# A decoder layer's cross-attention keys, from tokens on partitions to channels on partitions

## The reference, cut to what matters

```python
k = (encoder_hidden_states @ Wk + bk).reshape(b, se, NKV, HD).transpose(0, 2, 1, 3)   # NKV 4, HD 128
def _rmsnorm(x, w, eps=EPS):
    var = jnp.mean(xf * xf, axis=-1, keepdims=True)
    return (xf * jax.lax.rsqrt(var + eps)).astype(x.dtype) * w
k = _rmsnorm(k, kn_w)
scores = jnp.einsum('bhsd,bhed->bhse', q, k) * scale
```

## Time and profile before

| | |
|---|---|
| median of 3 runs | 1507.34 us (1504.46 to 1509.42) |
| the profiled execution, its own time | 1511.84 us |
| its span | 1510.0 us |
| PE busy | 1404.4 us, 93% of the span |
| DVE, ACT, POOL busy | 862.4 (57%), 715.8 (47%), 612.9 (41%) us |
| self-attention, about | 0 to 436 us of the span |
| cross-attention, about | 436 to 1290 us |
| one batch of the cross-attention | 51.2 us |

### The profile page before, as it was taken

The page is one execution under the profiler, slowest core; times in us unless marked ns, Lnnn a source line. Parts: engine busy times, 40 slices in busy tenths (PEclk is TensorE's granted clock), DMA queues, the critical chain, the costliest instruction groups (busy, mean ns, idle before and its releaser), DMA issues. The chain is left out here.

```text
span 1510.0 us, 24824 instructions
## 1 busy us (share of the span) xinstructions
PE 1404.4 (93%) x8553; PEld 1180.6 (78%) x8553; DVE 862.4 (57%) x3010; ACT 715.8 (47%) x1885; POOL 612.9 (41%) x936
## 2 busy tenths in 40 slices
PE   7889999999987999999999999999999997499976
PEld 7678988887866788888888888888888886377854
DVE  2644353434346676667666766676667665743357
ACT  3655555556335444445444544444444445343246
POOL 1221211212116455455545554555455436344164
PEclk9999999999999999999999999999999999599998
DMA  6211111212434221222122212212221221675363
GB/s 197 90 34 45 66 60 63 77 34 67 141 124 119 58 66 37 64 59 57 46 64 59 58 46 64 56 48 58 58 58 37 73 66 68 229 214 161 107 220 106
DMA packets 70548, 126.57 MB, mean 84 GB/s; under 512 B 11835, under 2 KB 47007, under 8 KB 69528
## 3 DMA queue, kind: packets, MB, share of 16 engines
q1 hardware_dynamic: 65848, 110.04, 23.9%
q0 software_dynamic: 4576, 14.95, 3.5%
HBM read 93.50 MB, written 31.45 MB: 83 GB/s over the span
## 5 line engine op out<-in xcount | busy, mean ns | idle before, releaser
L1341 POOL TENSOR_TENSOR b_pcarry<-b_half 128x1 f32<-128x1 f32 x173 | 49.2, 284 | 370.7 <-DVE b_rinv L1204 347.4
L75 PE MATMUL bank<-b_kTh,b_q 128*100 128x362 f32 x512 | 171.4, 336 | 8.2 <-POOL b_q L1362 6.1
L1085 ACT ACTIVATE b_probs<-b_probs,b_nmax 100x361 f32<-100x361 f32 x256 | 152.0, 594 | 18.9 <-DVE b_nmax L1198 18.6
L1198 DVE CUSTOM_DVE_ANT_0 b_probs<-bank,b_mask 100x361 f32<-100x361 f32 x256 | 135.3, 529 | 44.5 <-issue 40.0
L1373 POOL TENSOR_SCALAR b_probs<-b_probs,b_rinv 100x361 f32<-100x361 f32 x256 | 148.2, 590 | 0.0
L1080 ACT ACTIVATE b_pTh<-bank 121x400 fp32r<-121x400 f32 x192 | 96.8, 505 | 101.7 <-PE bank L917 96.9
L1191 DVE TENSOR_TENSOR b_pTl<-bank,b_pTh 121x400 fp32r<-121x400 f32 x192 | 109.6, 571 | 56.9 <-ACT b_pTh L1080 56.9
L1133 ACT ACTIVATE b_oTh<-bank,b_bv 128x400 fp32r<-128x400 f32 x64 | 38.1, 595 | 211.3 <-PE bank L75 211.3
L431 ACT ACTIVATE a_probs<-a_probs,a_nmax 100x100 f32<-100x100 f32 x256 | 93.2, 367 | 46.8 <-DVE a_nmax L551 46.7
L917 PE MATMUL bank<-ident,b_probs 100*121 100x100 f32 x768 | 110.6, 266 | 4.4 <-POOL b_probs L1373 3.5
L917 PEld LDWEIGHTS bank<-ident,b_probs 100*121 100x121 f32 x768 | 108.2, 187 | 6.6 <-POOL b_probs L1373 4.4
(11 more groups left out here) (255 smaller groups left out, 3871.0 us busy)
## 6 DMA issues: line engine op xcount, KB each, us to landing
q_d<-a_qb SPq DMA_DIRECT2D x64, 200.0 KB, 2.3
b_q_raw<-q_d SPq DMA_DIRECT2D x64, 200.0 KB, 2.4
b_q_raw<-rs_d SPq DMA_DIRECT2D x64, 200.0 KB, 3.4
b_ctxr<-in_ctxT SPq DMA_DIRECT2D x48, 242.0 KB, 4.8
y_d<-c_y SPq DMA_DIRECT2D x32, 256.0 KB
c_Eraw<-in_expert_w SPq DMA_DIRECT2D x10, 512.0 KB, 6.8
a_stage<-in_Wq SPq DMA_DIRECT2D x4, 1024.0 KB
stage<-in_Wo SPq DMA_DIRECT2D x8, 512.0 KB, 4.6
```

The costliest lines, as they stand in the source:

```text
L75: mm = eng.matmul(out, lhsT=l(c), rhs=r(c), start=first and k == 0, stop=last and k == n - 1)
L1085: act.activation(p, p, ACT.Exp, scale=-1.0, bias=nmax[:, s % 2, h:h + 1], accum_out=psums[:, s % 2, h:h + 1]).then_inc(e_rdy, 1)
L1198: dve.tensor_tensor_reduce(out=probs[:, s % 2, h, 0:SE], in0=s_bank[h % 2][0:S, 0:SE], in1=mask_s[:], scale=-1.0, scalar=BIG, op0=ALU.add, ...
L1341: pool.tensor_tensor(pcarry[:, k:k + 1], half_s[:, 0:1], half_s[:, 0:1], ALU.add)
```

## The change

It makes the keys with channels on partitions. For each of the four key heads, 128 columns of `Wk` are stationary and the context of all three chunks, 362 columns, moves: 4 heads of 12 products. The context's halves are laid out so that the three chunks adjoin. The steps are then:

- PE: head 0 at the end of slot 1, heads 1 and 2 in the quarters of slot 2, head 3 behind them; `key_sums` at the end of slot 2 sums the squares of the four heads over the partitions with a column of ones into four strips of bank 5. There are no key transposes, and the first score of each slot waits for one head of keys instead of all.
- DVE: `key_bias` moves each head from PSUM to SBUF with its bias; `key_newton` (two instructions, slot 3) makes a Newton step on the root; `key_scale` multiplies each head by the spread roots; `keys_lo`. Heads 0 and 1 of batch j+1 are scaled in slot 3, heads 2 and 3 in slots 0 and 1 of batch j+1 itself.
- ACT: `key_square` per head; `key_root` (Ln, Exp, Square; first in slot 3); `keys_hi` per head; `context_hi`, moved here from POOL, for chunks 0 to 2 behind the exponents of heads 0 to 2 in slot 1.
- POOL: no powers and no high halves; `context_lo` of all three chunks between `normalise(j, 0)` and `normalise(j, 1)`.
- SP: `spread_key_roots` behind `load_q(4j+4)`: four stores of one row each to DRAM, a wait until they have landed, and four loads that spread one row each over 128 partitions.

In the self-attention the query roots get the same Newton step (one more ACT and two DVE instructions for every four heads), the sums of squares go into bank 5 and stand behind the fourth query head, and PE's wait for the logarithm ahead of the output product is replaced by one for the Newton step ahead of every fourth query head. The queries' scale takes in the factor that the Newton steps leave. The keys of batch 0 are made at the end of the self-attention as before, in the new layout; seven dummy products ahead of a transpose in the first batch go with it. Bias, buffers and semaphores are changed to suit and are not all shown.

```diff
...
+                if m % XG == XG - 1 and XG <= m <= TAIL:
+                    pe.wait_ge(nw_set, m // XG)
...
-                if ss_bank(u) is not bank[6]:
-                    pe.wait_ge(ln_set, u - 1)
+                if ss_bank(u) is bank[5]:
+                    pe.wait_ge(sq_set, XG * u + XG + 2)
+                else:
+                    pe.wait_ge(sq_set, XG * u + XG)
+                    pe.wait_ge(nw_set, u - 1)
                 for r in range(XG):
-                    mm = pe.matmul(ss_bank(u)[r * SHD:(r + 1) * SHD, 0:GT], lhsT=ones_s[:], rhs=qsq[:, (XG * u + r) % SQ],
+                    mm = pe.matmul(ss_bank(u)[r * SHD:(r + 1) * SHD, 0:GT], lhsT=ones_s[:], rhs=square_tile(XG * u + r),
...
-                if m[0] is not None:
-                    square_sums(m[0] // XG)
                 if m[3] is not None:
                     query_head(m[3])
                 if m[0] is not None:
-                    pe.wait_ge(ln_set, m[0] // XG + 1)
+                    square_sums(m[0] // XG)
...
                     act.wait_ge(ss_done, (m - SQ) // XG + 1)
-                act.activation(qsq[:, m % SQ], q_bank(m)[:, 0:GT], ACT.Square, bias=bq_s[:, m % XH:m % XH + 1]).then_inc(sq_set, 1)
+                act.activation(square_tile(m), q_bank(m)[:, 0:GT], ACT.Square, bias=bq_s[:, m % XH:m % XH + 1]).then_inc(sq_set, 1)
             def roots(u):
...
+            def newton(u):
+                dve.wait_ge(rt_set, u + 1)
+                dve.scalar_tensor_tensor(out=qrt[:], in0=ss_bank(u)[:, 0:GT], scalar=rms_eps_s[:, 0:1], in1=qrt[:],
+                                         op0=ALU.add, op1=ALU.mult).then_inc(nw_set, 1)
+                dve.wait_ge(nw_set, u + 1)
+                dve.scalar_tensor_tensor(out=qrs[:], in0=qrt[:], scalar=-3.0, in1=qrs[:], op0=ALU.add, op1=ALU.mult).then_inc(qrs_set, 1)
...
+            def spread_key_roots(jn):
+                sp.wait_ge(k_rs, jn + 1)
+                for kv in range(XKV):
+                    sp.dma_start(kr_d[jn, kv].unsqueeze(0), krs[kv * SHD:kv * SHD + 1, :]).then_inc(krs_out, 16)
+                sp.wait_ge(krs_out, 16 * XKV * (jn + 1))
+                wait(sp, k_rdy, XKV * jn)
+                for kv in range(XKV):
+                    sp.dma_start(krb[:, kv], kr_d[jn, kv].partition_broadcast(P)).then_inc(k_in[kv], 16)
...
                     load_q(4 * j + 4, 0, 16 * j + 12)
+                    spread_key_roots(j + 1)
...
+            def keys(jn, kv, chunks=range(DC)):
                 if chunks[0] == 0:
-                    pe.wait_ge(ctx_lo, 3 * jn + c + 1)
-                    if c < 2:
-                        wait(pe, v_lo, 3 * (jn - 1) + c + 2)
-                    elif not (isinstance(jn, int) and jn == 0):
-                        pe.wait_ge(k_ev, 3 * jn + 2)
-                mm = product3(pe, key_bank(jn, c)[0:KT, :], lambda i: ctxh[:, c, i, :],
-                              lambda i: ctxl[:, c, i, :], lambda i: Wkh[:, i, :], lambda i: Wkl[:, i, :],
+                    if kv == 0:
+                        pe.wait_ge(ctx_lo, 3 * (jn + 1))
+                        pe.wait_ge(v_lo, 3 * jn)
+                    if kv >= 2:
+                        pe.wait_ge(k_sq_set, 4 * jn + kv - 1)
...
+            def key_sums(jn):
+                pe.wait_ge(k_sq_set, XKV * (jn + 1))
                 for kv in range(XKV):
-                    mm = pe.transpose(kv_bank[KEY_T_BANK[c]][:, kv * KT:(kv + 1) * KT],
-                                      kn[:, c % 2, kv * XHD:(kv + 1) * XHD], ident_s[0:KT, 0:KT])
-                mm.then_inc(kt_done, 1)
+                    mm = pe.matmul(kv_bank[0][kv * SHD:(kv + 1) * SHD, 0:SEQ], lhsT=ones_s[:], rhs=k_sq[:, jn % 2, kv, 0:SEQ],
...
                     if s >= 2 and first:
                         pe.wait_ge(w_lo, KV_PIECES + 2 * (s - 1))
                     if s == 2:
+                        if not last:
+                            keys(j + 1, 3)
                         output(j, 0, range(1))
-                        if not last:
-                            transpose_keys(j + 1, 0)
-                            if first:
-                                values_product(n - 1, s - 1, j)
-                            keys(j + 1, 2)
                     if s == 3:
                         output(j, 1, range(1, 2))
-                    if before and not (first and s == 2):
+                    if before:
                         values_product(n - 1, (s + 3) % 4, j)
+                    if s == 2 and not last:
+                        key_sums(j + 1)
...
                     if s == 3:
-                        if not last:
-                            transpose_keys(j + 1, 1)
-                            transpose_keys(j + 1, 2)
...
+            def key_square(jn, kv):
+                act.wait_ge(k_ev, XKV * jn + kv + 1)
+                act.activation(k_sq[:, jn % 2, kv, 0:SEQ], key_bank(jn, kv)[:, 0:SEQ], ACT.Square,
+                               bias=bk_s[:, kv:kv + 1]).then_inc(k_sq_set, 1)
+            def key_root(jn):
+                act.wait_ge(k_ss, jn + 1)
+                wait(act, krs_out, 16 * XKV * jn)
+                act.activation(krs[:], kv_bank[0][:, 0:SEQ], ACT.Ln, bias=rms_eps_s[:, 0:1]).then_inc(k_ln, 1)
+                act.wait_ge(k_ln, jn + 1)
+                act.activation(krs[:], krs[:], ACT.Exp, scale=-0.5).then_inc(k_root, 1)
+                act.wait_ge(k_root, jn + 1)
+                act.activation(k_sq[:, jn % 2, 0, 0:SEQ], krs[:], ACT.Square).then_inc(k_rt, 1)
+            def keys_hi(jn, kv):
+                act.wait_ge(k_rdy, XKV * jn + kv + 1)
+                act.activation(kTh[:, jn % 2, kv, 0:SEQ], k_raw[:, jn % 2, kv, 0:SEQ], ACT.Copy).then_inc(kt_hi, 1)
+            def context_hi(jn, c):
+                act.wait_ge(ctx_in[c % 2], ctx_loads(jn, c))
+                act.wait_ge(v_done, 3 * (jn - 1) + c + 1)
+                act.activation(ctxh[:, :, c * KT:(c + 1) * KT], ctxr[:, c % 2], ACT.Copy).then_inc(ctx_hi, 1)
...
+                    if s == 3 and not last:
+                        key_root(j + 1)
...
                             exponent(j, s, h)
+                        if s == 1 and not last:
+                            context_hi(j + 1, h)
+                    if s == 2 and not last:
+                        key_square(j + 1, 1)
                     if now:
                         queries_hi(n + 1)
+                        if s == 3 and not last:
+                            keys_hi(j + 1, 0)
                         exponent(j, s, 3)
                     if first:
                         for k in range(2):
                             split_hi(KV_PIECES + 2 * s + k)
+                    if s == 1 and not last:
+                        key_square(j + 1, 0)
+                    if s == 2 and not last:
+                        key_square(j + 1, 2)
+                        key_square(j + 1, 3)
...
-                    if s in (2, 3) and not last:
-                        keys_hi(j + 1, s - 2, 1 - par)
+                    if s < 2 and now:
+                        keys_hi(j, s + 2)
                     if s == 3 and not last:
-                        keys_hi(j + 1, 2, 1 - par)
+                        keys_hi(j + 1, 1)
...
+            def key_bias(jn, kv):
+                dve.wait_ge(k_done, XKV * jn + kv + 1)
+                dve.tensor_scalar(k_raw[:, jn % 2, kv, 0:SEQ], key_bank(jn, kv)[:, 0:SEQ], bk_s[:, kv:kv + 1], None,
+                                  ALU.add).then_inc(k_ev, 1)
+            def key_newton(jn):
+                t = k_sq[:, jn % 2, 0, 0:SEQ]
+                dve.wait_ge(k_rt, jn + 1)
+                dve.scalar_tensor_tensor(out=t, in0=kv_bank[0][:, 0:SEQ], scalar=rms_eps_s[:, 0:1], in1=t,
+                                         op0=ALU.add, op1=ALU.mult).then_inc(k_nw, 1)
+                dve.wait_ge(k_nw, jn + 1)
+                dve.scalar_tensor_tensor(out=krs[:], in0=t, scalar=-3.0, in1=krs[:], op0=ALU.add, op1=ALU.mult).then_inc(k_rs, 1)
+            def key_scale(jn, kv):
+                dve.wait_ge(k_in[kv], 16 * (jn + 1))
+                k_ = k_raw[:, jn % 2, kv, 0:SEQ]
+                dve.tensor_tensor(k_, k_, krb[:, kv], ALU.mult).then_inc(k_rdy, 1)
+            def keys_lo(jn, kv):
+                dve.wait_ge(kt_hi, XKV * jn + kv + 1)
+                dve.tensor_tensor(kTl[:, jn % 2, kv, 0:SEQ], k_raw[:, jn % 2, kv, 0:SEQ],
+                                  kTh[:, jn % 2, kv, 0:SEQ].bitcast(F32), ALU.subtract).then_inc(kt_lo, 1)
...
                             probs_lo(n - 1, h)
+                        if s == 3 and h == 0 and not last:
+                            key_newton(j + 1)
                     if s == 0 and routed(j):
                         keep_logits(j - 2)
+                    if s == 2 and not last:
+                        key_bias(j + 1, 1)
                     if now:
                         queries(n + 1)
+                        if s == 3 and not last:
```

(37 more changed lines are left out.)

200 lines of the change are left out of this document (85 added, 115 removed).

## The result

The changed kernel takes 1667.03 us (median, 1665.94 to 1667.23), the kernel before 1505.9 beside it: ratio 1.1067, 95% interval 1.1042 to 1.1091. The forecast was 1625, the range 1560 to 1670: the sign and the two chains were right, the size was 42 us too small. The measured time lies 3 us inside the range, and outside the 1595 to 1660 that the forecast case had for itself. The profiled execution has a span of 1663.6 us against 1510.0.

A forecast was written before the change was run, and what follows sets the result against it. PE was taken as the bound, busy 50.35 of 51.20 us per batch. Per batch +8.15 over 15 batches gave +122; 1511.8 + 122 + 2 - 4 = 1632, adjusted to the median 1627, stated as 1625, range 1560 to 1670.

The forecast's parts named there:

- the two chains: Cross-attention batch: key roots through DRAM in slot 3 (wait 5.8 us) and the context's third chunk in slot 1 (2.7).
- the forecast case: Whole kernel: both waits and one clock loss per batch, 1625 us, own bounds 1595 to 1660, chance 0.60.
- PE work: Each cross-attention batch: key products -0.26, transposes gone -2.74, sums added +0.95, together -2.05 us.
- Third chunk: Slot 1: load waits for the first low half, delaying POOL; PE waits 2.7 us, bounds 1.7 and 4.0.
- Roots through DRAM: Slot 3: DVE waits for the roots' store and broadcast, delaying POOL, then PE by 5.8 us; bounds 4.5 and 6.6.
- The clock: Behind PE's waits: one 3.4 us half-speed stretch per batch, costing 1.7 us; bounds 0 and 3.4.
- Self-attention: Added ACT and DVE instructions, covered by PE's output product: 2 us in all, up to 16 x 1.85 = 30 uncovered.
- The start: Start of the cross-attention: long waits for normalised keys and dummy products go, -4 us, range -8 to +4.
- (d): Every batch: clock lost twice and waits at upper bounds, +11.9 us per batch, 1685 us; chance 0.06.
- (a): Every batch: same waits at lower bounds, clock stays up, +4.15 us per batch, 1567 us; chance 0.22.
- (b): DVE's first key scaling: broadcasts arrive before DVE asks, PE not held, 1472 or about 1485 us; chance 0.09.
- PE's second largest wait: Sign: PE's largest waits are for POOL's queries' low half and probabilities, at the start of slots 0 and 2.

The follow-up runs named there:

- e9: e7 without the key roots' Newton step, and head 1's key scaling and splitting moved from slot 3 to the next batch's slot 0: 1502.62 us, ratio 0.9923.
- e4: Changed kernel plus unused TensorE products, 12 ahead of head 0's keys in slot 1 and 16 at the end of slot 3: 1602.98 us, ratio 1.0669.
- e7: Changed kernel with key scaling later in slot 3, context chunks rounded earlier, the self-attention part undone and the key root's chain tightened: 1509.01 us, ratio 1.0036.
- e2: Changed kernel with ScalarE rounding context chunks 0 and 1 in slot 0 and chunk 2 at the start of slot 1: 1595.33 us, ratio 1.0606.
- e1: Changed kernel with head 0's key scaling moved behind the fourth head's mask and both inversions in slot 3: 1608.87 us, ratio 1.0707.

## Why the prediction was right in sign and short in size

Per batch the forecast had -2.05 + 2.7 + 5.8 + 1.7 = +8.15. The trace has +10.0 in the batch shown (61.19 - 51.20) and +10.2 in the mean steady batch (61.4).

- **PE work, -2.05: right.** Three key products of 362 columns with 128 columns of weights start 0.167 us apart (743.05, 743.21, 743.38 in the trace), as taken from 100 columns. A set of sums costs 0.92 by the prediction's reckoning (750.80 - 749.53 - 0.18 - 0.17, from the product ahead of it to the second behind it), against 0.95. A wait costs PE about 0.16 us more than the profile calls idle (a product of 512 columns is recorded for 0.39 and costs 0.23), so the three waits of a steady batch (3.1 + 3.65 + 0.6) cost 7.8. Take them and the clock (4.35) off 61.4, and 49.2 is left, the forecast's 51.2 - 2.05 = 49.15. e9 agrees, whose clock stays up: 50.2 less 0.8 of waits is 49.4.
- **Third chunk, +2.7: right in cause, wrong in place, and right in size (3.0) by luck.** I had it at the probabilities of slot 2, behind POOL's normalising. PE already stands one step earlier, at the product of head 0 at the end of slot 1, which asks for all three low halves (`ctx_lo` at 3(jn+1)). Slot 2 then has no wait. The chain itself came as forecast: the last low half ended 9.1 us behind the start of slot 1, where I had 9.2. But I added 3.6 us of POOL work that PE doesn't wait for, and took PE to want the result 3.6 us later than it does (from 732.83 to the end of slot 1 are 5.3 us, less 1.7 of low clock, my estimate). The two errors cancel.
- **Roots through DRAM, +5.8: right in mechanism, too high; 4.3 of idle time measured (3.7 + 0.6), which costs 4.6, at the lower bound of 4.5.** Counted from the first score product (750.55), the Newton step ended at +3.9 (said +4.2), the broadcasts were issued at +5.9 (said +7.5), the first had landed at +9.2 (said +10.5), the reciprocal came at +10.1 (said +11.4). The term that failed is the store: 2.0 us from the first of four issues to the first load, where I had 1.0 for the issues plus 2.3 for the landing. The issues were right (the fourth starts 0.86 behind the first), so the last store landed within 1.14 us of its issue. The row I took the 2.3 from (q_d, 200 KB) moves far more bytes than a root row of 1.4 KB. POOL's query part took 1.68, not the 1.05 of the lower bound.
- **The clock, +1.7: the step that failed most; 4.35 measured, above my upper bound of 3.4.** I read one stretch of 3.4 us behind a wait of 1.49 and took it, once per batch, for the price of all waiting. Behind the wait at slot 0 the stretch is twice as long, and the one in slot 1 has its own. Over 15 batches that is 40 us short. e4, which leaves both gaps in place and removes the lower clock, shows the price by itself.
- **Self-attention, +2: failed, 10.4 measured.** I named PE's output product as the cover for the added instructions and said the residual starts later, but did not follow SP: the query roots' store was moved later, and a load was queued behind it. That is 4.3 of it. Another 3.3 are PE's own, around the new place of the sums, which I had at no cost. The bound of 30 held it.
- **The start, -4, came out near zero; a small part at the other end of the kernel stays open.** The first layer-norm of the cross-attention is 20.4 us later (551.4 against 531.0), of which 10.9 are the self-attention and 9.5 the first batch, so nearly like any other. The first batch's waits for the normalised keys did go, but PE now waits up to 6.5 us for the low half of the output weights, up to 4.0 for the squares of the keys and up to 5.1 for the context. Behind the last layer-norm the changed kernel is 6.9 us shorter (220.6 against 227.5), which I didn't look into.
- **The sum of the misses.** From profile to profile the span grew by 153.6 us, and the forecast had 120. The fifteen batches cost 149 in place of 122 (per steady batch +2.65 for the clock, -1.2 for the roots, +0.5 for the chunk; the first and the last have less), the self-attention 9 more, the start 4 more, the end 6 less: 34. The other 8 of the 42 aren't the kernel's. I took off 4.5 because the profiled execution before lay above its median, that of the changed kernel lay 1.1 below its own, and I rounded down by 2. That the time lies within the range owes something to luck: had the roots cost the 5.8 that I put, it would have been some 18 us longer and above 1670.
- **The page on DMA.** The Trainium skill, page "DMA: Bandwidth & Descriptors", section "Anatomy of one DMA — SWDGE (gpsimd) path", has a fixed 2.0 us per DMA. That section is on DMAs issued by GpSimd, and those here are issued by SyncE. The store doesn't agree: four small ones together took 2.0 us from the first issue, and the last of them at most 1.14. Nor does the prediction's estimate by its formula, 2.4 for a broadcast of 185 KB: the first of the four landed 3.3 us after the first issue, and the page of the profile has 3.7 as the median. The prediction's 3.0 was nearer.
- **The rivals.** (d), waits at their upper bounds and the clock lost twice, 1685, was the nearest in the clock; (a) had the roots' wait right and the clock wrong. (b) needed the roots back at +6, and they came at +9.2: with everything reordered, e7 reached only 1.0036, and e9, with 50.2 us per batch still 1.1 above the 49.15, 0.9923. Of the signs named beforehand that of PE's second largest wait failed (not slot 2's start, but the end of slot 1), and DVE stood 2.64 us ahead of the first scaling, where I had 3 to 4.

## What to carry to other kernels

A wait of TensorE can cost its length and the lower clock behind it: here 7.8 us of waits per batch cost 12.2, so about one and a half times their length. Count each wait separately. When a value must leave the chip and come back, put the instruction that meets it behind everything in its engine's queue that others wait for; here this alone gave back 54 of 161 us, without making the trip any shorter. And if a store is made to wait for one more step, read what is queued behind it on the issuing engine.

## What the runs showed of the hardware that I had not expected

- The stretches at 1.2 GHz come in two lengths, 3.4 and 6.8 us, and the wait ahead of them doesn't settle which. In the changed kernel 6.8 follow each of the twelve waits at slot 0 between 580 and 1290 us (3.4 to 3.95 us), and 3.4 each of the twelve in slot 1 (2.9 to 3.65). But in e2 nine waits at slot 0 of 3.4 to 4.0 us are followed by 6.8 and four of 3.4 to 3.7 by 3.4, and in e1 the pair of 1.3 and 0.7 is mostly followed by 3.4 and four times by nothing. What decides stays open.
- Idle time of TensorE can be filled with unused products at a gain: 28 per batch, some 6 us of them (3.55 us for sixteen at 689.16 in e4), made the kernel 60 us faster.
- DVE and POOL take longer where they run beside each other. A scaling of two SBUF tiles takes 0.52 to 0.54 us alone and 1.03 to 1.17 beside POOL's work, POOL's queries 1.38 instead of 1.05 and two of its normalisations 1.40 to 1.56 instead of 1.11, in e1 even 2.74. The Trainium skill, page "SBUF — State Buffer", section "🔬 SBUF: two separate sides", says that a VectorE operation with two SBUF inputs and a GpSimd operation that reads SBUF take one pair of ports in turn, each for a whole instruction; these rows agree as far as both get longer, and don't show who held the ports. Whether e9's 5 us come from it isn't shown.
